# Second attention of a two-layer network: ranks and places moved into the step of the choice, blank rows set by VectorE

## The chip, the cores and the metric

The kernel runs on one core of one Trainium2 chip. The metric is the device time of one execution in microseconds, as the median of several runs. One further execution was profiled, and all rows of the trace shown here come from it.

## What is computed

Two layers, each a mixer over the channels of eight 32x32 images (`B` = 8 images of `T` = 1024 tokens with `C` = 128 channels) and then a mixture of eight experts, of which each token takes two. The change lies in the second layer, in the stage that computes the linear attention and the routing of the tokens to the experts. Cut to what matters:

```python
# _L1_conv_ref, after the convolutions: linear attention, projection, batch norm
vk = jnp.einsum('bhds,bhes->bhde', v, k)
out = jnp.einsum('bhde,bhes->bhds', vk, q)
out = out[:, :, :-1] / (out[:, :, -1:] + EPS)
y = _conv(out, w_proj) * inv + shift              # added to x
# _L1_ffn_ref: layer norm, gate, the two best experts of each token
probs = jax.nn.softmax(layernorm(x) @ gate_w, axis=-1)
dispatch_w, expert_idx = jax.lax.top_k(probs, TOP_K)
out = sum over e of combine[:, e] * (gelu(x_norm @ w1[e] + b1[e]) @ w2[e] + b2[e])
```

The kernel does not compute all experts for all tokens. It writes each normalized token twice to DRAM, into the region of each of its two experts, and the next stage runs the experts over tiles of these regions. For this each token needs its rank among the tokens of its expert.

## The kernel before

The program is a row of stages with a barrier of all engines after each. The stage of the change is `attend_and_route` (line 1749 on). It works image by image in a software pipeline written out by hand. The order of the instructions on each engine is the order of the Python loops at the end of each engine's block; engines meet only in semaphores. Step `b` works on three images at once:

- `divide(b-1)` (VectorE, line 2085): numerator times reciprocal of the denominator, four halves of 512 columns. Its inputs come from `fractions(b-1)` (TensorE, line 1890; four pairs `num`, `den`) and `reciprocals(b-1)` (ScalarE, lines 1995 and 1997, Ln and Exp).
- `locate(b-3)` (VectorE, lines 2221 to 2230): seven short operations in a chain that turn the result of `ranks(b-3)` (TensorE, lines 1958 and 1960, nine bf16 matmuls of the mask) into the row numbers `places`. `places` has two buffers.
- `turn(b-2)` (TensorE, line 1942), `moments(b-2)` (VectorE, lines 2138 and 2142), `rstds(b-2)` (ScalarE, line 2027 on), `normalize(b-2)` (ScalarE, line 2045): transposes, layer norm and the rows that are to be sent.
- `mix(b)` (TensorE, lines 1900 and 1906), `copy_v(b)` (VectorE, line 2093), `rectify(b)` (ScalarE, lines 2006 and 2011): keys, values and queries of image b.
- `logits(b-2)` (TensorE, line 1950), `residual(b-2)` (VectorE, line 2162).
- `products(b)` (TensorE, line 1916) and `mask_products(b)` (VectorE, lines 2102 to 2105): the product of values and keys, tile `vk`.
- `choose(b-2)` (VectorE, lines 2177 to 2208, 19 short operations): the two best experts of each token, the mask and the gates; two exponentials in between come from ScalarE (`exponentials`, lines 2052 and 2054). The mask is ready at line 2197.
- `project(b-1)` (TensorE, line 1926), `scale(b-1)` (ScalarE, line 2021, tile `yb`), `add(b-1)` (VectorE, line 2111).

There are eleven steps (`b` = 0 to 10); the last holds only `ranks(7)` and `locate(7)`. Six banks of PSUM go round over all results of TensorE except the transposes, in the order of the list `order`: a result waits until the one six places before it in the list has been read. So `order` has to follow TensorE's program, and it decides which reader TensorE waits for.

GpSimd takes no part in the arithmetic. For each image it waits for the gates and the places (line 2291), then issues 16 indirect DMAs (line 2294) of 128 rows each; "the sends" below. Before the sends of image 5 it waits until the keys and values of the last image are out of the planes and sets a tile `blank` to zero with row numbers in it (lines 2281 to 2288). SyncE sends these blank rows to DRAM: seven DMAs as soon as they are set (line 1865), eight more when VectorE has planned the tiles after `locate(7)` (line 1870). VectorE's planning follows `locate(7)` directly. In steps 5 to 7 SyncE also loads the weights of the experts (lines 1858 to 1862). `normalize(b)` waits until the sends of image `b-2` have landed, since the rows have two buffers.

Of the kernel before, what the change touches and what calls it, by code (L numbers as in the profile page):

```python
# [13 lines left out]
B = 8  # L14
# [294 lines left out]
ROW = C + 2  # L309
G = T // C  # L310
SLOT = 256
SQ = SLOT // C
# [1436 lines left out]
def attend_and_route(nc, sb, sem, bank, w, X, planes, vkm0, ksm0, q_dram, xd_dram, table, resident, records):  # L1749
# [16 lines left out]
    shift = sb("shift", [C, 1], F32)  # L1766
    bn_log = sb("bn_log", [C, 1], F32)
    order = [("router", 0)]
    for b in range(B + 3):
        if 1 <= b <= B:  # L1770
            order += [(what, b - 1, i) for i in range(4) for what in ("num", "den")]
        if b >= 3:
            order.append(("ranks", b - 3))
        if b < B:
            order += [("ka", b, n) for n in range(2)] + [("va", b, n) for n in range(2)]
            order += [("qa", b, n) for n in range(2)]
        if 2 <= b < B + 2:
            order.append(("logits", b - 2))
        if b < B:
            order.append(("vk", b))  # L1780
        if 1 <= b <= B:
            order += [("proj", b - 1, n) for n in range(2)]
    banks = Banks(sem, tuple(range(6)), order)
    turned = Banks(sem, (6, 7), [("turn", b, n) for b in range(B) for n in range(2)])

    def dead(s, first, end):
        return planes[:, s].rearrange("c m n -> c (m n)")[:, first:end]

    rows = [dead(s, 0, 2 * G * ROW).rearrange("t (q k r) -> t q k r", q=G, k=2) for s in (2, 1)]
    blank = dead(2, 3 * T, 3 * T + BLANKS * SQ * ROW).rearrange("t (n r) -> t n r", n=BLANKS)  # L1790
# [37 lines left out]
    planned, blanks_sent, blank_ready, resident_loaded = sem("planned"), sem("blanks_sent"), sem("blank_ready"), sem("resident_loaded")  # L1828
# [18 lines left out]
    with nc.Block() as block:  # L1847
# [28 lines left out]
        def _(pe):  # L1876
# [43 lines left out]
            def project(b):  # L1920
                for n in range(2):
                    unit = ("proj", b, n)
                    pe.wait_ge(*banks.room(unit))
                    for m in range(2):
                        pe.wait_ge(*banks.emptied(("num", b, 2 * m + n)))
                        ins = pe.matmul(bank[:, banks.slot(unit), :], w["c_proj"][:, m * C:(m + 1) * C], o[:, 2 * m + n, :],
                                        start=(m == 0), stop=(m == 1))
                    ins.then_inc(banks.fills(unit), 1)

            def center_router():  # L1930
                pe.wait_ge(router_step, 2)
                pe.matmul(bank[:, banks.slot(("router", 0)), 0:E], w["centre"], scaled_router[:], start=True, stop=True)
                pe.matmul(bank[:, banks.slot(("router", 0)), E:2 * E], ln_bias[:], w["moe1_router"],
                          start=True, stop=True).then_inc(banks.fills(("router", 0)), 1)

            def turn(b):
                pe.wait_ge(added, 2 * b + 2)
                for n in range(2):
                    unit = ("turn", b, n)
                    pe.wait_ge(*turned.room(unit))  # L1940
                    for u in range(4):
                        ins = pe.transpose(bank[:, turned.slot(unit), u * C:(u + 1) * C], chunk(b, 4 * n + u), w["ident"])
                    ins.then_inc(turned.fills(unit), 1)
# [9 lines left out]
            def ranks(b):  # L1953
                unit = ("ranks", b)
                pe.wait_ge(*banks.room(unit))
                pe.wait_ge(mask_ready, b + 1)
                slot = banks.slot(unit)
                pe.matmul(bank[:, slot, 0:(G + 1) * E], w.before, mask[:, b % 2].rearrange("t q e -> t (q e)"), start=True, stop=False)
                for d in range(1, G + 1):
                    ins = pe.matmul(bank[:, slot, d * E:(G + 1) * E], w.ones,  # L1960
                                    mask[:, b % 2, 0:G + 1 - d, :].rearrange("t q e -> t (q e)"), start=False, stop=(d == G))
                ins.then_inc(banks.fills(unit), 1)

            pe.wait_ge(ones_set, 1)
            center_router()
            for b in range(B + 3):
                if 1 <= b <= B:
                    fractions(b - 1)
                if b >= 3:
                    ranks(b - 3)  # L1970
                if 2 <= b < B + 2:
                    turn(b - 2)
                if b < B:
                    mix(b)
                if 2 <= b < B + 2:
                    logits(b - 2)
                if b < B:
                    products(b)
                if 1 <= b <= B:
                    project(b - 1)  # L1980

        @block.scalar
        def _(act):
# [86 lines left out]
        def _(dve):  # L2070
# [36 lines left out]
            def add(b):  # L2107
                for n in range(2):
                    dve.wait_ge(*banks.emptied(("proj", b, n)))
                    cols = X[:, b * T + n * HALF:b * T + (n + 1) * HALF]  # L2110
                    dve.tensor_tensor(cols, cols, yb[:, n, :], ALU.add).then_inc(added, 1)
# [99 lines left out]
            def locate(b):  # L2211
                p, done = b % 2, [b * RANK]

                def then(ins):
                    ins.then_inc(located, 1)
                    done[0] += 1
                    dve.wait_ge(located, done[0])

                unit = ("ranks", b)
                dve.wait_ge(*banks.full(unit))  # L2220
                then(dve.tensor_tensor(s["slot"][:], bank[:, banks.slot(unit), 0:G * E].rearrange("t (q e) -> t q e", q=G),
                                       base[:].unsqueeze(1).to_broadcast([C, G, E]), ALU.add))
                then(dve.tensor_tensor(base[:], base[:], bank[:, banks.slot(unit), G * E:(G + 1) * E], ALU.add))
                dve.sem_inc(banks.frees(unit), 1)
                for k in range(2):
                    then(dve.tensor_tensor(s["at"][:], s["slot"][:], hot[p][k][:], ALU.mult))
                    then(dve.tensor_reduce(place[:, :, k:k + 1], s["at"][:], AX.X, ALU.add))
                if b >= 2:
                    dve.wait_ge(sent[p], b // 2 * SENDS)
                dve.tensor_copy(places[:, p], place[:]).then_inc(placed, 1)  # L2230
                dve.wait_ge(placed, b + 1)

            set_up()
            for b in range(B + 3):
                if 1 <= b <= B:
                    divide(b - 1)
                if b >= 3:
                    locate(b - 3)
                if 2 <= b < B + 2:
                    moments(b - 2)  # L2240
                if b < B:
                    copy_v(b)
                if 2 <= b < B + 2:
                    affine(b - 2)
                    residual(b - 2)
                if b < B:
                    mask_products(b)
                if 2 <= b < B + 2:
                    choose(b - 2)
                if 1 <= b <= B:  # L2250
                    add(b - 1)
            dve.wait_ge(added, 2 * B)

            done = [0]
# [22 lines left out]
        @block.gpsimd  # L2277
        def _(pool):
            for b in range(B):
                p = b % 2  # L2280
                if b == 5:
                    for what in ("ka", "va"):
                        pool.wait_ge(*banks.full((what, B - 1, 0)))
                        pool.wait_ge(*banks.full((what, B - 1, 1)))
                    pool.memset(blank, 0.0).then_inc(blank_ready, 1)
                    pool.wait_ge(blank_ready, 1)
                    pool.tensor_copy(blank.rearrange("t n (q r) -> t (n q) r", q=SQ)[:, :, ROW - 1:ROW],
                                     w["blank_rows"].unsqueeze(2)).then_inc(blank_ready, 1)
                pool.wait_ge(row_ends, 2 * b + 2)
                pool.wait_ge(placed, b + 1)  # L2290
                pool.sem_inc(held, 1)
                for q in range(G):
                    for k in range(2):
                        pool.indirect_dma_start(xd_dram, bass.IndirectOffsetOnAxis(places[:, p, q, k:k + 1], 0),  # L2294
                                                rows[p][:, q, k, :], None).then_inc(sent[p], 16)
            for p in range(2):
                pool.wait_ge(sent[p], B // 2 * SENDS)
# [173 lines left out]
```

## Time and profile before

| | us |
|---|---|
| median of 3 runs | 2483.74 |
| lowest and highest | 2478.91, 2508.16 |
| the profiled execution | 2497.49 |
| its span on the core | 2495.7 |
| mean granted TensorE clock in it | 0.887 of full |

The times of rows count from the start of the span. A row of the timeline gives start, duration, engine, line, operation, output and input tiles, how many instructions it merges, and, in brackets, how long the engine's idle time before it was and what the profile takes to have ended it. The name of a DMA there is that of the transfer which used the semaphore in another stage, so it need not be the transfer that is meant.

### The profile page before, as it was taken

The numbers are of one execution on the slowest core, as the hardware profiler recorded it, in microseconds if no ns is written. First come the engines' busy times: TensorE is split into PE (matmuls) and PEld (weight loads), VectorE is DVE, ScalarE is ACT, GpSimd is POOL, SyncE is SP. The second block draws the span as 40 slices with busy tenths as digits, with TensorE's granted clock in tenths as the row PEclk, the third lists the DMA queues.
The fourth block names the chain that finished last, engine by engine and source line by source line (L and its number), as shares of the span: only waits on it lengthen the run. The fifth ranks groups of instructions, "written<-read, shape, count | busy, mean of one in ns | idle before, by whom it ended". The sixth has DMA issues, their size and how long they took to land. (4 is left out here: it accounts for less than half of the span.)

```text
span 2495.7 us, 41218 instructions
## 1 busy us (share of the span) xinstructions
PE 2001.1 (80%) x13306; PEld 1095.7 (44%) x13307; DVE 1432.0 (57%) x3154; ACT 1092.8 (44%) x1682; POOL 756.2 (30%) x883
## 2 busy tenths in 40 slices
PE   5759999898989898986587885996668872599994
PEld 2321233232222222223466774564446541488883
DVE  4779888787868687613154555652245444244444
ACT  4530666565656565672133331451134331244343
POOL 1240003333332424243244442000003445344442
PEclk9865999999999999996798997999988885799996
DMA  3844132323232231012323334202111321233225
GB/s 130 205 169 68 18 52 26 60 27 60 27 60 34 53 43 44 20 36 72 91 82 82 84 83 156 80 34 61 31 34 41 108 63 45 76 84 82 77 74 213
DMA packets 134781, 179.99 MB, mean 72 GB/s; under 512 B 44592, under 2 KB 87856, under 8 KB 132336
## 3 DMA queue, kind: packets, MB, share of 16 engines
q1 hardware_dynamic: 116208, 138.25, 23.3%
q0 software_dynamic: 18432, 39.88, 4.8%
q8 instruction: 86, 1.41, 0.2%
q14 instruction: 55, 0.45, 0.1%
HBM read 99.04 MB, written 69.01 MB: 67 GB/s over the span
## 5 line engine op out<-in xcount | busy, mean ns | idle before, releaser
L775 DVE TENSOR_REDUCE mx<-bank 128x1 f32<-128x512 f32 x1024 | 640.6, 699 | 143.4 <-PE bank L546 96.4
L722 ACT ACTIVATE P<-bank 128x1024 f32<-128x1024 f32 x512 | 498.4, 1022 | 404.6 <-PE bank L648 321.5
L546 PE MATMUL bank<-ks,qs 96*128 96x512 bf16 x1024 | 373.9, 414 | 58.7 <-DVE mx L775 51.2
L1286 POOL DMA_INDIRECT results<-yo,places x284 | 274.3, 966 | 364.0 <-DVE yo L1276 289.2
L1202 PE MATMUL bank<-xt,up 128*128 128x256 f32 x1136 | 293.6, 404 | 58.5 <-DVE xt L1256 31.2
L648 PE MATMUL bank<-qs,ks 99*128 99x512 bf16 x1024 | 310.0, 387 | 11.6 <-ACT P L722 6.6
L628 PE MATMUL bank<-P,vt 128*32 128x512 f32 x2048 | 278.0, 615 | 1.6 <-issue 1.6
L2294 POOL DMA_INDIRECT dispatched<-planes,places x128 | 124.1, 969 | 483.9 <-DVE stats L2138 365.9
L1202 PEld LDWEIGHTS bank<-xt,up 128*128 128x128 f32 x1136 | 214.5, 199 | 99.6 <-issue 60.1
L546 PEld LDWEIGHTS bank<-ks,qs 96*128 96x128 bf16 x1024 | 100.7, 99 | 302.9 <-DVE mx L775 212.8
L648 PEld LDWEIGHTS bank<-qs,ks 99*128 99x128 bf16 x1024 | 77.2, 97 | 296.5 <-ACT P L722 186.0
L1233 ACT ACTIVATE hidden<-bank,rec 128x256 f32<-128x256 f32 x284 | 121.0, 475 | 177.0 <-PE bank L1202 154.0
L995 POOL TENSOR_TENSOR a<-o,den 128x512 f32<-128x512 f32 x32 | 40.5, 1267 | 333.8 <-ACT den L710 309.2
L1211 PE MATMUL bank<-planes,hidden 128*128 x1136 | 139.2, 276 | 0.8 <-issue 0.7
L1238 ACT ACTIVATE gate<-bank,rec 128x256 f32<-128x256 f32 x142 | 65.6, 474 | 165.1 <-PE bank L1202 134.2
L1045 POOL DMA_INDIRECT dispatched<-outgoing,places x128 | 124.2, 970 | 44.9 <-issue 41.7
L1211 PEld LDWEIGHTS bank<-planes,hidden 128*128 128x128 f32 x1136 | 133.2, 193 | 1.3 <-issue 1.2
L1271 DVE TENSOR_TENSOR y<-bank,rec 128x256 f32<-128x256 f32 x142 | 60.0, 423 | 123.3 <-PE bank L1211 94.0
L1722 PE MATMUL bank<-planes,bands 32*32 32x240 f32 (+2 forms) x3840 | 84.7, 398 | 42.7 <-issue 24.0
L1265 DVE SCALAR_TENSOR_TENSOR hidden<-bank,rec,gate 128x256 f32<-128x256 f32 x142 | 67.0, 482 | 86.1 <-PE bank L1202 35.3
L1743 DVE STREAM_TRANSPOSE planes<-out 128x1024 f32<-128x1024 f32 x24 | 43.6, 1880 | 98.6 <-ACT out L1735 98.6
L1185 PE MATMUL bank<-weights,xr 128*128 128x128 f32 x284 | 57.3, 285 | 43.2 <-DMA xr<-dispatched 42.8
(298 smaller groups left out, 2609.5 us busy)
## 6 DMA issues: line engine op xcount, KB each, us to landing
xr<-dispatched SPq DMA_DIRECT2D x142, 130.0 KB
y<-results SPq DMA_DIRECT2D x64, 256.0 KB
qk_parts<-parts SPq DMA_DIRECT2D x16, 768.0 KB, 5.1
qs<-qk_parts SPq DMA_DIRECT2D x84, 128.0 KB
ks<-qk_parts SPq DMA_DIRECT2D x84, 128.0 KB
v_turned<-vt SPq DMA_DIRECT2D x8, 1024.0 KB, 5.6
vt<-v_turned SPq DMA_DIRECT2D x8, 1024.0 KB
bands<-toeplitz SPq DMA_DIRECT2D x16, 320.0 KB, 2.9
```

The source lines that it names most:

```text
L546: pe.matmul(bank[:, slot, :], qs[par][0:KB, h, c * C:(c + 1) * C], ks[par][0:KB, h, half * HALF:(half + 1) * HALF], start=True, stop=True) ...
L628: ins = pe.matmul(bank[32 * j:32 * j + 32, 4, :], vt[:, par, s, head * VH:(head + 1) * VH], P[:, (2 * e + j // 2) % SLOTS, j % 2 * HALF:(j ...
L648: ins = pe.matmul(bank[:, 2 * pair + u, :], ks[par][:, head, s * C:(s + 1) * C], qs[par][:, head, n * HALF:(n + 1) * HALF], start=True, st ...
L722: act.activation(P[:, x % SLOTS, :], bank[:, 2 * pair:2 * pair + 2, :] .rearrange("p a t -> p (a t)"), ACT.Exp).then_inc(probs_ready, 1)
L775: dve.tensor_reduce(mx[:, k // 2, k % 2:k % 2 + 1], bank[:, slot, :], AX.X, ALU.max).then_inc(unit_freed, 1)
L1045: pool.indirect_dma_start(xd_dram, bass.IndirectOffsetOnAxis(places[:, q, k:k + 1], 0), outgoing[:, q, k, :], None).then_inc(sent, 16)
L1202: ins = pe.matmul(bank[:, 2 + f, 0:SLOT], up[:, p, f * C:(f + 1) * C], xt[:, p, :], start=True, stop=True)
L1211: ins = pe.matmul(bank[:, 6 + p, q * C:(q + 1) * C], hidden[:, p, f, q * C:(q + 1) * C], weights(e, W2 + f * C), start=(f == 0), stop=(f = ...
L1233: act.activation(hidden[:, p, f, :], bank[:, 2 + f, 0:SLOT], ACT.Gelu, bias=rec[:, r, f:f + 1]).then_inc(h_ready, 1)
L1286: pool.indirect_dma_start(yd_dram, bass.IndirectOffsetOnAxis(places[:, p, q:q + 1], 0), yo[:, p, q, :], None).then_inc(sent[p], 16)
L1722: ins = pe.matmul(sums[:, :, y0:y1], bands[rows, m * TAPS + dy, :], plane[:, :, y0 + dy - PAD:y1 + dy - PAD], start=(dy == DY_ORDER[0]), s ...
L2294: pool.indirect_dma_start(xd_dram, bass.IndirectOffsetOnAxis(places[:, p, q, k:k + 1], 0), rows[p][:, q, k, :], None).then_inc(sent[p], 16)
```

## The change

`ranks` and `locate` of an image go from the beginning of the step after the choice (behind `fractions` and `divide` of that step) to the end of the step of the choice (behind `project` and `add`). On TensorE `ranks(b-2)` now stands between `project(b-1)` and the next step's `fractions(b)`; on VectorE `locate(b-2)` stands between `add(b-1)` and `divide(b)`. The order of the PSUM banks follows. The eleventh step goes. The zeroing of `blank` and its row numbers leave GpSimd and its wait, and VectorE does them after `locate` in step `b` = 8.

```diff
-    for b in range(B + 3):
+    for b in range(B + 2):
         if 1 <= b <= B:
             order += [(what, b - 1, i) for i in range(4) for what in ("num", "den")]
-        if b >= 3:
-            order.append(("ranks", b - 3))
...
             order += [("proj", b - 1, n) for n in range(2)]
+        if b >= 2:
+            order.append(("ranks", b - 2))
...
-            for b in range(B + 3):
+            for b in range(B + 2):
                 if 1 <= b <= B:
                     fractions(b - 1)
-                if b >= 3:
-                    ranks(b - 3)
...
                     project(b - 1)
+                if b >= 2:
+                    ranks(b - 2)
...
-            for b in range(B + 3):
+            for b in range(B + 2):
                 if 1 <= b <= B:
                     divide(b - 1)
-                if b >= 3:
-                    locate(b - 3)
...
                     add(b - 1)
+                if b >= 2:
+                    locate(b - 2)
+                if b == B:
+                    dve.memset(blank, 0.0).then_inc(blank_ready, 1)
+                    dve.wait_ge(blank_ready, 1)
+                    dve.tensor_copy(blank.rearrange("t n (q r) -> t (n q) r", q=SQ)[:, :, ROW - 1:ROW],
+                                    w["blank_rows"].unsqueeze(2)).then_inc(blank_ready, 1)
...
-                if b == 5:
-                    for what in ("ka", "va"):
-                        pool.wait_ge(*banks.full((what, B - 1, 0)))
-                        pool.wait_ge(*banks.full((what, B - 1, 1)))
-                    pool.memset(blank, 0.0).then_inc(blank_ready, 1)
-                    pool.wait_ge(blank_ready, 1)
-                    pool.tensor_copy(blank.rearrange("t n (q r) -> t (n q) r", q=SQ)[:, :, ROW - 1:ROW],
-                                     w["blank_rows"].unsqueeze(2)).then_inc(blank_ready, 1)
```

## Rows read from the trace of the kernel before

**Rows 1.** Windows of the stage: its steps 2 to 8, and what follows

```profile
core 0: us, PE busy (x) PEld busy (x) DVE busy (x) ACT busy (x) POOL busy (x), PEclk, DMA share, GB/s
1860.00:1883.70 23.70, 23.70 (x101) 16.33 (x100) 14.62 (x58) 13.58 (x29) 0.00 (x0) 0.93 0.08 23
1883.70:1917.00 33.30, 27.15 (x114) 17.66 (x112) 16.34 (x65) 13.61 (x29) 15.51 (x16) 0.93 0.17 55
...
1949.90:1983.40 33.50, 28.23 (x110) 18.35 (x109) 16.37 (x64) 13.37 (x29) 15.58 (x16) 0.81 0.14 46
...
2016.40:2053.60 37.20, 28.03 (x112) 18.12 (x110) 16.45 (x64) 13.60 (x29) 19.16 (x18) 0.84 0.30 84
2053.60:2076.40 22.80, 14.78 (x65) 9.99 (x64) 15.83 (x67) 9.64 (x22) 11.76 (x13) 0.77 0.10 33
2076.40:2115.00 38.60, 4.18 (x26) 4.03 (x25) 10.37 (x53) 4.97 (x14) 19.15 (x20) 0.50 0.11 36
```

**Rows 2.** Timeline, step 2, in which nothing is sent

```profile
1873.40 2.61 PE L1916 MATMUL bank<-vT,kT 128*128 128x129 f32 x16
1876.20 0.28 DVE L2102 COPY vk<-bank 128x129 f32<-128x129 f32 x1
```

**Rows 3.** Timeline, step 5 and the beginning of step 6: sends, product, choice, scale, adds

```profile
1958.52 0.96 POOL L2294 DMA_INDIRECT dispatched<-planes,places  x1 [13.37 <-DVE places L2230]
1965.15 3.79 PE L1916 MATMUL bank<-vT,kT 128*128 128x129 f32 x16
1972.15 0.30 DVE L2102 COPY vk<-bank 128x129 f32<-128x129 f32 x1 [4.11 <-DMA y<-results]
1976.34 0.23 DVE L2197 TENSOR_TENSOR mask<-best,second 128x64 bf16<-128x64 f32 x1
1977.70 0.96 POOL L2294 DMA_INDIRECT dispatched<-planes,places  x1 [0.30 <-issue]
1979.93 0.78 ACT L2021 ACTIVATE yb<-bank,shift,inv 128x512 f32<-128x512 f32 x1 [4.41 <-issue]
1982.20 0.69 DVE L2111 TENSOR_TENSOR X<-X,yb 128x512 f32<-128x512 f32 x1 [0.77 <-ACT yb L2021]
1988.21 0.21 DVE L2221 TENSOR_TENSOR slot<-bank,base 128x64 f32<-128x64 f32 x1
1989.79 0.17 DVE L2230 CAST places<-place 128x16 uint32<-128x16 f32 x1
1990.00 1.68 DVE L2138 BATCH_NORM_STATS2 stats<-bank 128x6 f32<-128x128 f32 x8
1990.80 0.96 POOL L2294 DMA_INDIRECT dispatched<-planes,places  x1 [12.13 <-DVE places L2230]
1993.33 1.14 POOL L2294 DMA_INDIRECT dispatched<-planes,places  x1 [0.30 <-issue]
```

**Rows 4.** All copies of the product (line 2102): what ended VectorE's idle time

```profile
  DMA bands<-toeplitz: 18.9, 2
  DMA y<-results: 16.7, 3
```

**Rows 5.** Timeline, after step 8: sends of image 6, rest of image 7

```profile
2076.31 3.79 PE L1950 MATMUL bank<-router,X 128*128 128x8 f32 x16
2088.60 0.89 DVE L2138 BATCH_NORM_STATS2 stats<-bank 128x6 f32<-128x128 f32 x4 [8.12 <-remote]
2100.38 0.96 POOL L2294 DMA_INDIRECT dispatched<-planes,places  x1 [0.30 <-issue]
2106.30 2.64 DVE L2162 TENSOR_SCALAR X<-bank,scale,shift 128x128 f32<-128x128 f32 x8 [11.00 <-DMA y<-results]
2114.89 0.17 DVE L2230 CAST places<-place 128x16 uint32<-128x16 f32 x1
```

**Rows 6.** Zeroing on GpSimd (timeline); on VectorE elsewhere (instruction groups)

```profile
2044.73 3.36 POOL L2285 MEMSET planes<- 128x3900 f32 x1
L927 DVE MEMSET a<- 128x1040 f32 x4 | 3.7, 925 | 36.4 <-DMA dispatched<-a 36.0 <-DVE table L970 0.3 <-issue 0.2
```

## The prediction

> **What bounds the kernel now.** I read the page first. TensorE is busy 80% of the span, but that is an average over eleven stages, and the change touches one. So I took windows over that stage, cut at the first `divide` of each step [rows 1]. Here the reader is to see two things. Step 2, in which nothing is sent, takes 23.7 us and TensorE is busy in all of it. Steps 3 and 5 have the same work and the 16 sends of an image, and take 33.3 and 33.5 us; the five steps 3 to 7 go from 1883.7 to 2053.6, that is 169.9 us, or 34.0 each. TensorE is busy in only 26 to 28 us of each. Something costs some 9 us a step, and no engine's busy time accounts for it.
>
> Next the timeline of two steps, to find where the 9 us are. In step 2 the product of values and keys ends on TensorE at 1873.40 + 2.61 = 1876.01, and VectorE copies it at 1876.20 [rows 2]. In step 5 it ends at 1965.15 + 3.79 = 1968.94, and VectorE, idle for 4.11 us, copies it only at 1972.15: 3.2 us late [rows 3]. ScalarE's `yb` waits for the projection, which follows the product directly, and starts after 4.41 us of idle time, 1.27 us after the last send has been issued (1977.70 + 0.96 = 1978.66; `yb` at 1979.93). The profile names nothing real for either ("issue", the name of another stage's DMA). The view of the line of the copy says the same of all of them: the five with a foreign name waited 35.6 us in total [rows 4]. After step 8, where sends of images 5 and 6 run back to back, it is plainer: the logits of image 7 end at 2080.10, and `residual` starts at 2106.30, 5.0 us after the last send of image 6 (2101.34). The moments stop for 8.12 us in the middle [rows 5]. The columns of these windows show GpSimd busy only with the sends [rows 1].
>
> I read this as follows: while the sends run, other engines' signals reach their readers late, and the last of them arrives when the sends are over. The trace does not name the mechanism; it shows the coincidence in all steps with sends and its absence in step 2. So the stage is bound by a ring: `yb` → `add` → `divide` → `locate` → 16 sends → `yb`.
>
> **The ring, term by term** [rows 3], from one first `yb` (1979.93) on: to the end of the second `add` 1982.20 + 0.69 - 1979.93 = 2.96; the four divides up to `locate` 1988.21 - 1982.89 = 5.32; `locate` 1988.21 to 1989.96 = 1.75; to the first send 0.84; 16 sends, 20.1 (those of image 2: 1958.52 to 1978.66 = 20.14); to the next `yb` 1.3. Together 32.3, which leaves 1.2 of step 5's 33.5 over: the ring explains the length of the step to within that.
>
> **What the change does to it.** `locate` goes ahead of the divides, so the 5.32 leave the ring: 2.96 + 1.75 + 0.84 + 20.1 + 1.3 = 27.0 us. Instructions are the same, seven on VectorE and nine on TensorE a step; none is added.
>
> What the moved parts delay:
> - TensorE's `ranks` now wait for the mask (ready at 1976.57) with the next `fractions` behind them. Before, two pairs could run ahead of the mask, right behind the projection. But the third pair needs a bank that `yb` frees, and ScalarE can't start its reciprocals before both `yb` (the second add starts at 1982.20). Two pairs need about 3.5 us, so the first is done by 1979: hidden by `yb`. If `yb` came as early as the mask, up to 3.5 us would show.
> - `locate` holds the divides by 1.75 us, and the last pair's bank is freed by the first divide. I put that at 0.9 us later for the last divide, against 1.75 that `locate` no longer takes behind it: the moments start 0.8 us earlier.
> - The other ring, through arithmetic alone, is step 5 without its two waits: 33.5 - 3.2 - 4.4 - 0.8 = 25.1 us, below 27.0. So the sends stay the bound.
> - The sends now start 5.3 us earlier relative to the work of the other engines. Before, they began 0.8 us after the moments; the product ended 10.4 us into them. Now it ends about 16 us in, and the logits, which end where the product starts, about 12 instead of 6.6. If the logits' signal is then held to the end of the sends as well, the ring is 25.7 (end of the sends) + `residual` 2.64 + copy of the product to the second exponential 3.37 (1979.93 - 4.41 - 1972.15) = 31.7 us.
>
> What is held and how long has no row for this order, so I bound a step by 27.0 and 31.7, with 28.5 for the case that the wait after the sends is 2.8 us instead of 1.3. I take 30.1, halfway between 28.5 and 31.7, because the tail shows logits held [rows 5] and steps 3 to 7 don't. Five steps: 169.9 - 5 x 30.1 = 19.4 us saved (34.9 to 11.4 between the bounds).
>
> **The end of the stage.** From the adds of step 7 (2053.6) to the end of `locate(7)` (2114.89 + 0.17 = 2115.06) it is 61.5 us now. After the change: sends of image 5 from 2.6 to 22.7, step 8 takes its 22.8 [rows 1], sends of image 6 from 23.6 to 43.7 (before 47.7), `residual` again 5.0 later, and 2115.06 - 2106.30 = 8.8 from there: 57.5. Saved: 4.0. If nothing is held here, up to 20.
>
> **Blank rows.** GpSimd loses 3.36 us of zeroing and a short copy, which lay in its idle time between two images: worth nothing. VectorE gets them: 925 ns for 1040 columns elsewhere makes 3.5 us for 3900 [rows 6], after `locate(6)`. Ahead of the last moments VectorE waits long anyway (8.12 us for half of them) [rows 5]; I cost it at nothing, 3.7 if that cover goes. SyncE's seven blank transfers start some 25 us later and lie under the sends of image 6; nothing but the end of the stage waits for them.
>
> One send at the time of VectorE's value copy takes 1.14 us instead of 0.96 [rows 3]. The Trainium skill (SBUF — State Buffer, the "DVE blocks DMA" trap) says that GpSimd can't write descriptors while VectorE runs in a mode with two ports. The row agrees in direction, with 0.18 us, and by the rule alone a step would not change; only if the new zeroing ran in such a mode, it would push the sends of image 6 by its length.
>
> **Sum.** 2497.49 - 19.4 - 4.0 = 2474.1 for a profiled execution. The median of the runs is 13.75 below the profiled one: 2460.
>
> **Rivals.**
> - *No change that counts* (0.18). The late signals are not tied to the sends but to TensorE's own pace (its clock is at 0.81 in step 5 and 0.93 in step 2). Then they move with the work, and only the 0.8 us a step is left: 2480. Against it: step 3 has a clock of 0.93 too and is as long as step 5. For it: nothing in the profile says that the sends hold the signals, they only coincide. The Trainium skill (SBUF — State Buffer, Who interferes with whom) states that TensorE and ScalarE never wait on anyone and that a DMA never contends with a compute engine. By that rule the sends couldn't be what is late, and this rival would hold; rows 4 and 5 speak against it.
> - *Slower* (0.12). With more of the work under the sends, logits or keys are held, and as long beyond the sends as in the tail: 31.7 + 5.0 = 36.7 us a step, 13.6 more in five, and the zeroing uncovered, 3.7: 2501. It decides where a step passes 34.0, that is, where signals are held over 2.3 us beyond the sends from the logits on.
> - *Much faster* (0.10). Steps at 27.0 and nothing held in the tail: 35 + 20 = 55 saved, 2429. Against it: rows 5.
> - My forecast (0.60): 2437 to 2478.
>
> **Chances.** Two per cent of 2484 is 50 us, about what a measurement of this kernel can tell from no change: faster than 2434 or slower than 2533. Only half of the third rival reaches the first, 0.05; for the second the slower rival would have to be three times as bad, 0.01. Within: 0.94. The range leaves out half of the much faster case and most of the slower one: 2436 to 2490; the forecast's own is 2437 to 2478.
>
> **What would show it.** Right: steps of 28 to 31 us between the first divides; sends of an image starting about 2.6 us after the second add; the first send of image 0 in step 2, before the divides of step 3; `yb` within 3 us of the last send or sooner. Logits prompt: steps near 27; logits held: `residual` starts at the end of the sends. Wrong: steps stay at 33 though the sends start 5 us earlier, and `yb` comes long after the last send; or `fractions` behind `ranks` make ScalarE's reciprocals wait. For the end: `residual` of image 7 near 49 us after the adds of step 7, and the zeroing (3.5 us on VectorE) inside its idle time.

## The result, and the profile after

The changed kernel is slower: 2516.95 us against 2499.02 us in the median of 22 runs each, a ratio of 1.007 with a 95% interval from 1.0049 to 1.009. The forecast was 2460 us, a gain of about 1.0% on the 2483.74 us of the three runs it had. The measured loss of 0.7% is small, but its interval leaves no room for a gain.

The windows of the stage, cut again at the first `divide` of each step (steps 2 to 8, then the rest). Columns as in [rows 1].

```profile
core 0: us, PE busy (x) PEld busy (x) DVE busy (x) ACT busy (x) POOL busy (x), PEclk, DMA share, GB/s
1866.00:1891.30 25.30, 25.30 (x110) 17.68 (x109) 16.00 (x64) 13.50 (x28) 0.00 (x0) 0.87 0.07 22
1891.30:1930.60 39.30, 25.53 (x109) 18.34 (x108) 16.28 (x64) 13.62 (x28) 15.96 (x17) 0.78 0.12 41
1930.60:1969.30 38.70, 26.01 (x111) 18.45 (x110) 16.20 (x65) 13.72 (x28) 15.50 (x17) 0.78 0.14 42
...
2045.70:2085.00 39.30, 26.83 (x112) 18.87 (x111) 16.18 (x64) 13.84 (x28) 16.18 (x17) 0.78 0.21 56
2085.00:2117.00 32.00, 15.83 (x59) 10.36 (x58) 14.21 (x59) 10.24 (x22) 14.37 (x16) 0.74 0.11 34
2117.00:2140.70 23.70, 4.20 (x26) 4.05 (x25) 13.90 (x55) 4.95 (x14) 15.31 (x16) 0.50 0.27 85
```

Steps 3 to 7 take 193.7 us (1891.3 to 2085.0), 38.7 each, against 169.9 and 34.0 [rows 1]: 23.8 more. Step 2 holds a `locate` now and takes 25.3 instead of 23.7. From the end of step 7 to the end of `locate(7)` it is 55.7 us instead of 61.5. Together 19.6 us more in the stage, close to the 17.9 between the medians. TensorE is busy for 25.7 us of a step, no more than the 27.4 before, and idle for 13.0 us instead of 6.6. So the new time is waiting, not work.

Where the time goes shows in the timeline at the end of step 3 and in step 4 (ScalarE, VectorE, TensorE, GpSimd; columns as before):

```profile
1929.96 0.95 POOL L2291 DMA_INDIRECT dispatched<-planes,places  x1 [17.97 <-DVE places L2230]
...
1935.39 3.74 PE L1900 MATMUL bank<-weights,planes 128*128 128x128 f32 x32
1939.59 0.58 ACT L2006 ACTIVATE kT<-bank 128x512 f32<-128x512 f32 x1
1940.68 1.12 PE L1950 MATMUL bank<-router,X 128*128 128x8 f32 x5
1944.19 0.39 PE L1950 MATMUL bank<-router,X 128*128 128x8 f32 x1 [1.24 <-issue]
...
1948.89 0.96 POOL L2291 DMA_INDIRECT dispatched<-planes,places  x1 [0.30 <-issue]
1949.89 0.60 ACT L2006 ACTIVATE kT<-bank 128x512 f32<-128x512 f32 x1 [9.72 <-DMA y<-results]
1952.68 0.89 PE L1950 MATMUL bank<-router,X 128*128 128x8 f32 x4 [1.23 <-issue]
1952.83 1.29 DVE L2093 COPY vT<-bank 128x512 f32<-128x512 f32 x2 [13.91 <-DMA y<-results]
1954.26 3.38 PE L1916 MATMUL bank<-vT,kT 128*128 128x129 f32 x16 [0.69 <-DVE vT L2093]
```

TensorE has made all keys and values by 1939.13. ScalarE reads the first half of the keys at 1939.59 and gets the second only at 1949.89, VectorE the values at 1952.83, 13.7 us late and 3.0 us after the last send (1948.89 + 0.96 = 1949.85). The logits themselves, 3.8 us before for the same work [rows 5], now crawl from 1940.68 to 1953.57. In the kernel before it was the product and the projection that were late [rows 3], not the keys and values.

The trace also stores when a semaphore was counted up, which none of the views prints. It settles on whose side the delay lies. TensorE's last pass for the second half of the keys ends at 1937.35, and its semaphore is counted up at 1949.87, 12.5 us later; the next four of TensorE's counts stand at 1952.73, 1952.83, 1952.87 and 1952.91, in the order of the work. Outside of the sends such a count follows the end by 0.01 to 0.02 us. So the readers react at once, and the signal itself is late. ScalarE's count at 1940.18, in the middle of this, came 0.01 us after its instruction.

The zeroing took what was costed:

```profile
2117.67 3.31 DVE L2253 MEMSET planes<- 128x3900 f32 x1 [0.88 <-DVE places L2230]
2121.02 0.20 DVE L2255 COPY planes<-weights 128x30 f32<-128x30 f32 x1
```

The last `locate`, 16.5 to 23 us into the sends of image 6, did not. It took 6.55 us instead of the 1.76 of all the others of this trace, and the waits in it are for VectorE's own signals: `slot` (line 2221) ends at 2134.36, and its semaphore is counted up at 2136.74.

```profile
2134.15 0.21 DVE L2221 TENSOR_TENSOR slot<-bank,base 128x64 f32<-128x64 f32 x1
2136.77 0.16 DVE L2223 TENSOR_TENSOR base<-base,bank 128x8 f32<-128x8 f32 x1 [2.41 <-DMA qk_parts<-parts]
```

### The profile page after: what moved, and what is told of

The parts are those of the page before. It is cut to its first block and busy times, and to the rows that moved or that the text cites. A ratio compares the mean times of both kernels' runs of the same rounds, so it can differ in the third digit from the quotient of the medians.

```text
span 2528.5 us, 41216 instructions
## 1 busy us (share of the span) xinstructions
PE 2012.9 (80%) x13306; PEld 1115.3 (44%) x13307; DVE 1435.3 (57%) x3156; ACT 1096.2 (43%) x1682; POOL 749.4 (30%) x881
## 5 line engine op out<-in xcount | busy, mean ns | idle before, releaser
L1202 PE MATMUL bank<-xt,up 128*128 128x256 f32 x1136 | 304.3, 415 | 77.5 <-DVE xt L1256 50.7
L1202 PEld LDWEIGHTS bank<-xt,up 128*128 128x128 f32 x1136 | 220.9, 205 | 120.9 <-issue 84.1
L1722 PE MATMUL bank<-planes,bands 32*32 32x248 f32 (+2 forms) x3840 | 86.0, 403 | 40.9 <-issue 22.8
```

Of the source, the lines that this page charges most:

```text
L1202: ins = pe.matmul(bank[:, 2 + f, 0:SLOT], up[:, p, f * C:(f + 1) * C], xt[:, p, :], start=True, stop=True)
L1722: ins = pe.matmul(sums[:, :, y0:y1], bands[rows, m * TAPS + dy, :], plane[:, :, y0 + dy - PAD:y1 + dy - PAD], start=(dy == DY_ORDER[0]), s ...
```

## The experiments

Theory A, from the profile of before and of after: indirect DMAs hold TensorE's signals, and the earlier sends now cover the keys and values. Theory B: the blank rows. Theory C: the new order on TensorE and VectorE by itself.

**One part alone.** `order_only` is the changed kernel with the blank rows left on GpSimd, `blank_only` the kernel before with nothing but them moved.

```diff
 # order_only, against the changed kernel: on GpSimd, ahead of the sends of image 5
+                if b == 5:
+                    ...
+                    pool.memset(blank, 0.0).then_inc(blank_ready, 1)
 # blank_only, against the kernel before: on VectorE, at the end of step 8
+                if b == B:
+                    dve.memset(blank, 0.0).then_inc(blank_ready, 1)
```

> Only the moves of ranks and locate and the order of the banks; the blank rows stay on GpSimd. Theory A (TensorE's signals are held while the sends run, and the earlier sends now cover the keys and values instead of the product): all of the loss is here, steps 3 to 7 at about 38 to 39 us as in the changed kernel, time 15 to 24 us over the kernel before. Theory B (the blank rows on VectorE, or their late transfers on SyncE, cost the time): within 5 us of the kernel before.

> Only the blank rows go to VectorE, at the end of step 8; ranks and locate stay where they were. Theory A: steps stay at 34.0 us on average, the time within 5 us of the kernel before, perhaps 1 to 3 us more or less at step 7 and in the tail. Theory B: 15 to 20 us slower.

Measured: `order_only` 1.0076 of the kernel before (1.0036 to 1.0117), `blank_only` 0.9989 (0.9958 to 1.0019). Steps 3 to 7 take 38.7 us each in `order_only` and 34.4 in `blank_only`. Theory B falls: the moves of ranks and locate carry the loss in the steps, and in the medians all of it that can be measured. The profiles leave one thing open. From the end of step 7 to the end of `locate(7)`, `order_only` takes 42.3 us (2061.31 to 2103.57) where the changed kernel takes 55.7. In the new order the blank rows on VectorE may cost something there: the 3.5 us of zeroing and the slow last `locate`, 4.8 us, are part of the 13.4. Each is one execution, so this is not shown. In `order_only` the values are late in the same way:

```profile
1928.08 1.29 DVE L2093 COPY vT<-bank 128x512 f32<-128x512 f32 x2 [13.72 <-DMA y<-results]
```

**The place of the sends.** `sends_late` and `sends_after_vk` are the changed kernel with one wait more on GpSimd.

```diff
 # sends_late
+                if b + 2 < B:
+                    pool.wait_ge(*banks.emptied(("num", b + 2, 3)))
 # sends_after_vk
+                if b + 3 < B:
+                    pool.wait_ge(*banks.full(("vk", b + 3)))
```

> The changed kernel with one more wait on GpSimd: the sends of image b start only when divide(b+2) has read its last bank, which is where they started before. Ranks, locate, banks and blank rows are as changed. Theory A (the position of the sends decides): steps 3 to 7 fall from 38.7 us to 32 to 34, the time is 5 us above to 10 us below the kernel before. Theory C (the order on TensorE and VectorE decides: fractions behind ranks behind the mask, the divides behind locate): the steps stay at 38 to 39 us and the time 15 to 20 us above the kernel before.

> The changed kernel with the sends of image b held back until the product of values and keys of image b+3 is done on TensorE (images 0 to 4; the others as changed). They then run beside the choice, the adds, the divides and the moments, where TensorE does little. Theory A: little of TensorE's work is signalled late, steps of 27 to 31 us, 15 to 35 us below the kernel before. If any 20 us of sends costs the same wherever they lie, steps of 33 us or more and the time of the kernel before. Theory C: 38 to 39 us a step.

Measured: `sends_late` 1.0105 (1.0068 to 1.0142), `sends_after_vk` 0.9997 (0.9955 to 1.0039). Neither did what theory A said. With the sends back in their place the steps fall to 36.4 us, not to 33, and two with loads on SyncE stay at 39.9 and 39.5; the keys are prompt again, but the product is now read 19 to 23 us after the first send, not 14 to 22. The ratio is even above the 1.0076 of `order_only`, measured beside it, though the intervals overlap; by the time alone (26.5 us above the kernel before in the medians) this run speaks for theory C. So place is not all. Behind the product the sends reach into the next step's keys:

```profile
1907.07 0.96 POOL L2293 DMA_INDIRECT dispatched<-planes,places  x1 [0.30 <-issue]
...
1910.46 1.09 ACT L2006 ACTIVATE kT<-bank 128x512 f32<-128x512 f32 x2 [2.14 <-DMA bands<-toeplitz]
```

Steps 4 to 7 take 32.4 to 34.9 us there. But step 3, in which nothing is sent until the product, takes 25.1. So even here 20 us of sends cost a step some 8 us. Directly behind `locate` they cost 13.6 (38.7 against 25.1), and in `sends_late` 11 or more. The place sets the price, and none of the three tried takes it away; this much of theory A holds.

**What in a send it is.** Four kernels add work to steps 0 to 2 of the kernel before, in which nothing is sent: 44 indirect DMAs like the sends, 44 plain ones from GpSimd, 88 plain ones from SyncE, and 110 zeroings of a tile on GpSimd.

```diff
 # extra_indirect, ahead of GpSimd's loop over the images
+            for n in range(44):
+                pool.indirect_dma_start(scratch[n], bass.IndirectOffsetOnAxis(index[:, 0:1], 0),
+                                        w.all[:, 0:ROW], None).then_inc(extra, 16)
 # extra_direct
+                pool.dma_start(scratch[n], w.all[:, 0:ROW]).then_inc(extra, 16)
 # extra_sync, ahead of SyncE's third load
+                        sp.dma_start(scratch[n], w.all[:, 0:ROW]).then_inc(extra, 16)
 # extra_busy
+                pool.memset(idle_tile[:], 0.0).then_inc(extra, 1)
```

> The kernel before, with 44 more indirect DMAs of the same size (128 rows of 520 bytes, from a constant tile into scratch tensors) that GpSimd issues from the start of the stage, some 55 us at the pace of the sends, over steps 0 to 2, in which nothing was sent. Theory A (sends hold TensorE's signals): steps 1 and 2, 17.4 and 23.6 us before, become 25 us and more, and logits or keys are read late. If the length of steps 3 to 7 has another cause (their work, the third image in them), steps 1 and 2 keep their times within 1 us.

> The same with 44 plain DMAs of the same shape from GpSimd's queue, no indices. If writing descriptors on GpSimd is what holds the signals, steps 1 and 2 grow as with the indirect ones, perhaps less since a plain DMA is issued faster. If the indices matter (GpSimd reads them), the steps stay at 17.4 and 23.6 us.

> The same transfers, 88 of them, issued by SyncE. If the traffic or the 16 completions of each DMA hold the signals, steps 1 and 2 grow by several us each. If it is GpSimd's part of a DMA, they stay within 1 us of 17.4 and 23.6.

> No DMA: GpSimd sets a tile of its own (128x512) to zero 110 times, one after the other, from the start of the stage, over some 50 us. If a busy GpSimd by itself slows the others (port or semaphores), steps 1 and 2 grow; theory A says they stay at 17.4 and 23.6 us within 1 us.

Each of the four ran once, under the profiler; they are read by their traces. Of `extra_indirect`, the timeline from its first to its last extra DMA, with the product, the first pair of `fractions` and their readers, then the first `divide`:

```profile
1816.43 0.96 POOL L2286 DMA_INDIRECT scratch<-weights,index  x1 [303.54 <-DVE index L2076]
1829.99 3.59 PE L1920 MATMUL bank<-vT,kT 128*128 128x129 f32 x16 [3.19 <-DVE vT L2098]
1834.28 1.02 PE L1894 MATMUL bank<-q,ksm 128*128 128x512 f32 x2
1861.50 0.29 DVE L2107 COPY vk<-bank 128x129 f32<-128x129 f32 x1 [31.65 <-DMA y<-results]
1870.83 0.96 POOL L2286 DMA_INDIRECT scratch<-weights,index  x1 [0.30 <-issue]
1872.70 0.69 ACT L1999 ACTIVATE rd<-bank,weights 128x512 f32<-128x512 f32 x1 [40.09 <-DMA bands<-toeplitz]
1874.08 0.69 DVE L2090 TENSOR_TENSOR o<-bank,rd 128x512 f32<-128x512 f32 x1 [11.76 <-issue]
```

The product of image 0 ends at 1833.58 and is read at 1861.50, 27.9 us late. The first pair of `fractions` ends at 1835.30, and ScalarE reads it at 1872.70, 37.4 us late. The first `divide` comes 57.7 us after the first extra DMA and 2.3 us after the last. For most of this time the stage stood still. Steps 1 and 2, for which the expectation was 25 us and more, took 22.2 and 24.7: step 0 had swallowed nearly all of the DMAs. Of `extra_direct`:

```profile
1828.78 23.39 POOL L2282 DMA_DIRECT2D scratch<-weights  x44 [299.60 <-POOLq L2329]
1840.03 1.95 PE L1918 MATMUL bank<-vT,kT 128*128 128x129 f32 x16
1842.02 0.29 DVE L2104 COPY vk<-bank 128x129 f32<-128x129 f32 x1 [2.81 <-PE bank L1918]
```

Same size, same queue, one every 0.53 us instead of 1.26, and the product is read 0.04 us after its end; the first `divide` comes at 16.3 us, step 1 takes 17.4. With SyncE's 88 DMAs and with the busy GpSimd it is the same: product read 0.03 us after its end, step 1 of 17.4 us. Step 2 takes 24.9, 22.5 and 23.4 us in the three, around the 23.6 of the kernel before. So it is neither the traffic, nor the completions, nor GpSimd being busy, but the indirect DMAs.

**Does it build up?** Theory D: a backlog grows over unbroken indirect DMAs, and a pause clears it. Theory E: whenever they run, signals are held.

```diff
 # pace4_after, pace4_before (behind each send; pace8_after: q % 4 == 3)
+                    if q % 2 == 1:
+                        pool.wait_ge(sent[p], b // 2 * SENDS + 32 * (q + 1))
 # halves, against the changed kernel
+                    if q == G // 2 and b + 3 < B:
+                        pool.wait_ge(*banks.full(("vk", b + 3)))
```

> The changed kernel; GpSimd waits after every fourth send until all of the image's sends so far have landed, then goes on. Theory D (a backlog builds up over some ten microseconds of unbroken indirect DMAs, and a pause lets the held signals through): the signals are read at most some 5 us late, a step is bound by the sends with their pauses (4 x about 8 us) or shorter, 28 to 33 us, the time 15 to 35 us below the changed kernel. Theory E (signals are held whenever indirect DMAs run, whatever the pauses): sends and pauses stretch over the whole step, steps stay at 38 us or grow.

> The same with a pause after every eighth send. Theory D: one pause in the middle, the hold of the first half ends there; steps of 30 to 34 us, 10 to 25 us below the changed kernel. Theory E: 38 to 40 us a step, no gain.

> The kernel before with the pause after every fourth send. Theory D: the product is read at once instead of 3 to 12 us late, steps of 27 to 31 us instead of 34.0, the time 10 to 30 us below the kernel before. Theory E: no gain, perhaps 3 to 5 us a step more, because the sends with their pauses end some 8 us later.

> The changed kernel with eight sends at once behind locate and eight more when the product of image b+3 is done on TensorE (images 0 to 4). The first eight (10 us) run beside the divides and moments and end as keys and values begin, the others beside the choice and the adds. Theories D and E both say that little is held: steps of 26 to 30 us, 20 to 40 us below the changed kernel and 5 to 25 below the kernel before. If the second half holds the next step's keys as 16 sends did (steps of 33 us there), the steps stay near 33.

| kernel | ratio to the kernel before | interval | steps 3 to 7, us |
|---|---|---|---|
| pace4_after | 0.9816 | 0.9751 to 0.988 | 25.9, 24.3, 24.4, 25.2, 25.3 |
| pace8_after | 0.9905 | 0.9871 to 0.994 | 34.9, 30.5, 31.9, 26.9, 36.4 |
| pace4_before | 0.989 | 0.9829 to 0.9952 | 25.1, 26.2, 25.1, 28.4, 27.5 |
| halves | 0.9942 | 0.9907 to 0.9977 | 29.0, 25.6, 32.7, 33.9, 32.3 |

Theory E falls: with a pause after every fourth send the steps of `pace4_after` are as short as its step 2 (25.5 us), in which nothing is sent, though the sends now fill nearly the whole step. Windows of steps 4 and 5 of `pace4_after`, then its timeline:

```profile
1880.90:1905.20 24.30, 24.10 (x110) 16.47 (x109) 16.19 (x65) 13.50 (x28) 14.99 (x16) 0.93 0.20 63
1905.20:1929.60 24.40, 23.98 (x110) 16.69 (x109) 16.13 (x64) 13.61 (x28) 13.55 (x15) 0.93 0.19 61
```

```profile
1914.28 1.29 DVE L2093 COPY vT<-bank 128x512 f32<-128x512 f32 x2 [1.23 <-DMA y<-results]
1918.41 2.96 PE L1916 MATMUL bank<-vT,kT 128*128 128x129 f32 x16
1921.40 0.29 DVE L2102 COPY vk<-bank 128x129 f32<-128x129 f32 x1
...
1927.56 1.14 POOL L2291 DMA_INDIRECT dispatched<-planes,places  x1 [1.62 <-DMA dispatched<-planes,places]
```

TensorE is busy in 24.1 of 24.3 us; the product is read 0.03 us after its end. Usual pauses are 1.6 us. Both kernels with pauses after every fourth gained about what theory D said or more. The mean step of `pace8_after`, 32.1 us, is in its range too: rows of eight unbroken sends (10 us) still hold something in most steps (the product is read 3.1 to 7.3 us late in four of the five). `halves` missed its range, with a mean of 30.7 us, and there the experiment was not what its edit says. From 1928.11 on, the second eight of an image run into the first eight of the next without a pause, so steps 5 to 7 (32.3 to 33.9 us) again have 16 unbroken sends; steps 3 and 4, mostly with eight, take 29.0 and 25.6.

**Onset, and what clears it.**

```diff
 # extra_paced, against extra_indirect; extra_16: range(16) instead of range(44)
+                if n % 4 == 3:
+                    pool.wait_ge(extra, 16 * (n + 1))
 # pause_busy, against the changed kernel, behind every fourth send
+                        for n in range(3):
+                            pool.memset(idle_tile[:], 0.0).then_inc(extra, 1)
+                            pool.wait_ge(extra, 3 * (b * G // 2 + q // 2) + n + 1)
```

> The kernel before with the 44 extra indirect DMAs of extra_indirect, which there moved the first divide from about 17 to 57.7 us after the start of GpSimd's DMAs, but with a wait for their landing after every fourth. Theory D (a backlog over unbroken sends): the first divide comes within 2 us of its usual place, 16 to 18 us after the start, and steps 1 and 2 take about 17.4 and 24 us though the DMAs run for some 70 us. Theory E (any indirect DMA holds signals while it runs): the first divide comes 30 us or more later than usual.

> The kernel before with only 16 extra indirect DMAs, unbroken, from the start of the stage. They end some 20 us after it. Theory D: nothing is late in the first 10 us, then the product of image 0 is held to the end of the 16 and the first divide comes some 25 us after the start instead of 17; steps 1 and 2 as usual (17.4 and 23 to 25 us). If the hold needs many more sends than 16, or the third image in the pipeline, the first divide is at 17 us.

> The changed kernel; after every fourth send GpSimd sets a tile of its own to zero three times (about 1.7 us), with no wait for a DMA. If the pause alone clears the backlog, the steps fall to 25 to 28 us and the time is that of pace4_after, 0.98 to 0.985 of the kernel before. If GpSimd has to stand in a wait, or the DMAs have to have landed, the steps stay near 38 us or between.

`extra_paced` and `extra_16` ran once each as well. Of `extra_16`, its product, the last extra DMA, and the copy of the product; of `extra_paced`, the same two:

```profile
1816.64 2.02 PE L1920 MATMUL bank<-vT,kT 128*128 128x129 f32 x16 [1.97 <-DVE vT L2098]
1822.09 0.96 POOL L2286 DMA_INDIRECT scratch<-weights,index  x1 [0.30 <-issue]
1825.77 0.29 DVE L2107 COPY vk<-bank 128x129 f32<-128x129 f32 x1 [9.27 <-DMA y<-results]
```

```profile
1812.47 1.95 PE L1920 MATMUL bank<-vT,kT 128*128 128x129 f32 x16
1814.46 0.29 DVE L2107 COPY vk<-bank 128x129 f32<-128x129 f32 x1 [2.81 <-PE bank L1920]
```

16 unbroken DMAs from 1803.1: the product, done 15.5 us later, is held for 7.1 us, to 2.7 us after the last of them. The first `divide` comes 24.1 us after their start, as expected (25); step 1 takes 19.7 us, 2.3 more than expected. With pauses, 44 of them hold the product for no time: the first `divide` comes 15.4 us after their start, step 1 takes 17.4 us and step 2 22.7. The same trace shows the reverse. The extra DMAs have delayed the sends of images 0 and 1, which then run as 32 in an unbroken row (1877.25 to 1917.73); the values made beside them are copied only at 1922.46, after 27.48 us of idle time of VectorE, and this step takes 52.4 us. `pause_busy` reaches 0.9881 (0.9847 to 0.9914) with steps of 24.8 to 26.4 us, and there GpSimd waits for no DMA: 2.0 us between two indirect DMAs, 1.7 of them filled with zeroing, are enough, and no wait for the landing is needed. Its ratio is a little above that of `pace4_after` (and above the 0.98 to 0.985 expected), with overlapping intervals.

**The other stage.** `pace4_both` is `pace4_after` with the same wait behind the sends of the first attention.

> pace4_after with the same wait after every fourth of the sends of the first attention (line 1045 on). If signals are held there too, a further 5 to 40 us below pace4_after (0.9816 of the kernel before); if GpSimd's longer time in the sends costs there (it also divides and normalizes in that stage), 5 to 15 us above it.

Measured 0.9839 (0.9749 to 0.9929) in four runs, no different from `pace4_after`. Of that stage it shows only that a pause there brings nothing that four runs can measure; the interval would hide 20 us either way.

## Why the prediction was wrong

- **That the sends hold the other engines' signals, and the rival that they don't.** Right for TensorE's signals, which `extra_indirect` shows in steps without sends; not for all engines alike. In the stage of the changed kernel none of ScalarE's counts that the trace stores is late, and of VectorE's only some in the last `locate` and just before it, by 0.4 to 2.4 us. The Trainium skill (SBUF — State Buffer, Who interferes with whom), cited beside the rival, says that TensorE and ScalarE never wait on anyone. As a rule on the ports of SBUF it may stand; as a guide to this kernel's time it doesn't, for 27.9 us of one signal's delay are measured here, with plain DMAs of the same queue at 0.04.
- **"32.3 ... the ring explains the length of the step to within that."** Here is the first error. It took the wait from the last send to `yb`, 1.3 us, for a constant of a ring, because it was 1.3 in two steps; over the five steps 3 to 7 it is 0.6, 1.2, 1.3, 2.8 and 5.8. The sum fitted, but the sends were not a link of fixed length; they were a window during which TensorE's signals pass late and in their order. [rows 3] show that they don't all wait for its end: the product was read at 1972.15, 6.5 us before the last send was issued. What counts is which signal is caught first. In the kernel before it was the product, then the projection; with the sends 5.3 us earlier it was the second half of the keys, after which residual, product, choice and `yb` still have to come.
- **"What is held ... so I bound a step by 27.0 and 31.7."** The step of the sum that failed. The worst case I allowed was that logits are held to the end of the sends. Measured are keys and values, held to 3.0 us beyond it: 38.7 us a step, where 30.1 was taken. The term "19.4 saved" is 23.8 lost. I had written that before "they began 0.8 us after the moments"; at that time the keys and values were all but made. I should have asked the same of the moved sends, which begin 5.4 us before the mixing (1929.96 and 1935.39).
- **The slower rival (0.12).** The right mechanism, at 36.7 a step and 2501 us; its clause "logits or keys" is what happened. Its size per step was 2.0 too small, its tail wrong. Its total, 17.3 us above the runs it had, comes close to the 17.9 measured by luck: in the stage, 10.2 us too little in the steps and 1.6 in step 2 are nearly made up by 9.5 too much at the end (3.7 lost forecast, 5.8 gained). By the profile the case for it was as good as for the forecast: [rows 5] showed logits held for 26 us.
- **The moved parts.** `fractions` behind `ranks` behind the mask cost little: in `pace4_after`, with the same order, a step takes 24.3 to 25.9 us, against 25.1 forecast for arithmetic alone. Once little is held, the change gains: `pace4_after` is 22.6 us below `pace4_before` in the medians of four runs each, measured side by side, and 11.0 in the stage by the profiles (222.3 against 233.3 us from the first copy of a product to `locate(7)`). The other half is not explained; the profiled execution of `pace4_after` is 17 us ahead at that first copy already, in code that is the same. Theory C falls with it.
- **The end of the stage.** 4.0 forecast, 5.8 measured, and the agreement is luck. Step 8 took 32.0 us and not "its 22.8", for most of the hold lay in `residual` of image 6 (12.77 us of idle time); `residual` of image 7 was hardly held and starts at 41.6 us after the end of step 7, not at 49; the last `locate` lost 4.8.
- **Blank rows.** Costed at nothing; `blank_only` measures 0.9989, in the old order. 3.31 us on VectorE for 3.5 forecast. In the new order the zeroing lay between `locate(6)` and the last moments with no wait to cover it, the case that the prediction priced at 3.7.
- **What to look for.** The first sign of being right, steps of 28 to 31 us, did not come. Of the sign of being wrong, half was seen: `yb` of step 4 starts at 1962.77, 12.9 us after the last send, but the steps did not stay at 33, they grew.

Not settled: what the indirect DMAs and TensorE's signals share, and whether the hold is as long when no profile is recorded. Whether the pauses matter or only the lower mean rate of sends that comes with them was not tested: no kernel spreads the sends evenly. Time since the first send is not all either: in the end of the changed kernel the result of `ranks(7)`, ready 16.3 us into the sends, is read after 0.2 us. Why `sends_late` holds the product longer than the kernel before, with the sends at the same distance from the moments, is open too.

## What to carry to other kernels

A wait that ends with another engine's long run is not a link of a chain but a window: before moving the run, list which signals fall into the new window, and forecast from the first of them. Long unbroken rows of indirect DMAs from GpSimd are such a window here; a pause of 1.6 us after every fourth costs GpSimd some 5 us an image (four gaps of 1.6 in place of 0.3) and gives back 7.5 us a step in the order of before (34.0 to 26.5) and 13.7 in the changed one (38.7 to 25.0). If a change should shorten a step and doesn't, look for engines that wait for an instruction which the trace shows as long done.

## What the runs showed of the hardware

- Indirect DMAs issued back to back on GpSimd (0.96 us each, one every 1.26 us, 128 rows of 520 bytes) make TensorE's signals late, from some 5 to 10 us after the first on. They come in the order of the work; the last comes some 3 us after the end of a row of 16 (2.9 in `extra_16`), 4.9 after 32 (the kernel before, [rows 5]), 6.5 after 44 (`extra_indirect`, ScalarE's second read at 1878.31). 44 of them held one signal for 37.4 us. 44 plain DMAs of the same shape on the same queue, 88 on SyncE's, and 64 us of zeroing on GpSimd held none.
- VectorE's own signals were late too, more rarely: the last `locate` of the changed kernel took 6.55 us instead of 1.76. None of ScalarE's was seen late there.
- TensorE itself slows under them: 16 passes of the logits took 12.9 us instead of 3.8.
- Pauses of 1.6 to 2.0 us after every fourth clear most of it, whether GpSimd waits or computes in them. After every eighth they help less (0.9905 against 0.9816).
- The best kernel of the study is the changed one with such pauses, `pace4_after`: 2430.25 us (four runs) where the kernel before took 2476.43, measured beside it.
